# Mask, shift and two layer norms on GpSimd, one exponential per batch, bounds loaded between products, and an earlier second preparation, in a decoder layer on one core

## The reference

```
S1 = S + a (k^T S);  S2 = exp(log_f) S1;  S3 = S2 + a (k^T S2) + k v^T;  o = q^T S3
```

## Time and profile before

| | |
|---|---|
| median of 3 runs | 2480.19 us (2478.8 to 2481.66) |
| the profiled execution | 2477.74 us, span 2476.0 us |
| mean granted TensorE clock | 0.828 |
| VectorE busy | 2113.5 us, 85% |
| TensorE busy | 1768.9 us, 71% |
| GpSimd busy | 1016.9 us, 41% |
| ScalarE busy | 777.2 us, 31% |

### The profile page before, as it was taken

One profiled execution on the slowest core, in us unless ns is written; L12 is line 12 of the kernel. 1 busy time (PEld: TensorE's weight loads), 2 busy tenths in 40 slices (PEclk: granted clock), 3 DMA queues, 4 the chain that ended last, 5 costly groups with the idle time before them and its releaser, 6 DMA issues.

```text
span 2476.0 us, 32575 instructions
## 1 busy us (share of the span) xinstructions
PE 1768.9 (71%) x9438; PEld 1338.2 (54%) x9438; DVE 2113.5 (85%) x5985; ACT 777.2 (31%) x2209; POOL 1016.9 (41%) x1164
## 2 busy tenths in 40 slices
PE   4258887988798879877988330367887568857893
PEld 2145666667566656665667210245575446745683
DVE  5999999999999999999999989999999989941000
ACT  2142145314531453145313100252223511234121
POOL 2503350465046504550564467353663653231103
PEclk7558998999799979998999665567998669976997
DMA  8000342334233423332335120000353003530243
GB/s 270 18 1 14 127 135 74 112 136 137 77 119 124 135 77 127 116 135 80 120 121 179 45 76 9 20 1 3 102 200 128 18 2 121 204 116 1 98 165 111
DMA packets 175116, 238.57 MB, mean 96 GB/s; under 512 B 28657, under 2 KB 148074, under 8 KB 174954
## 3 DMA queue, kind: packets, MB, share of 16 engines
q1 hardware_dynamic: 140874, 194.46, 23.2%
q10 hardware_dynamic: 27936, 25.44, 3.2%
q0 software_dynamic: 6144, 16.79, 2.1%
HBM read 202.09 MB, written 33.16 MB: 95 GB/s over the span
## 4 chain that ended last, share of the span: by engine, by line
DVE 53%; PE 18%; POOL 10%; issue 8%; ACT 8%; DMA 2%; SPq 0%; ACTq 0%; POOLq 0%; DVEq 0%; PEldq 0%
DVE ps L1548 10%; DVE ps L1529 9%; DVE prod L1521 8%; DVE terms L1536 6%; ACT probs L820 4%; PE ps L629 4%; DVE terms L1531 4%; PE ps L620 3%; PE ps L573 2%; PE ps L566 2%; DVE rec_out L1477 2%; DVE rec_in L1477 2%; DVE SE_out L1540 1%; POOL in_rows L1021 1%; PE ps L523 1%
## 5 line engine op out<-in xcount | busy, mean ns | idle before, releaser
L1548 DVE TENSOR_REDUCE ps<-terms 128x64 f32<-128x320 f32 x1024 | 447.8, 482 | 0.0
L1529 DVE TENSOR_REDUCE ps<-prod 128x16 f32<-128x272 f32 x1024 | 396.5, 431 | 0.0
L620 PE MATMUL ps<-xg,fc 128*128 128x128 f32 x2848 | 361.4, 288 | 29.9 <-PE ps L629 12.5
L1536 DVE TENSOR_TENSOR terms<-ps,rec_out 128x256 f32<-128x256 f32 x1024 | 380.7, 413 | 0.0
L1521 DVE TENSOR_TENSOR prod<-ps,rec_in 128x256 f32<-128x256 f32 x1024 | 380.4, 412 | 0.0
L620 PEld LDWEIGHTS ps<-xg,fc 128*128 128x128 f32 x2848 | 350.4, 203 | 52.8 <-issue 44.4
L629 PE MATMUL ps<-pj,hT 128*128 128x256 f32 x1424 | 341.9, 395 | 34.5 <-ACT hT L901 34.5
L629 PEld LDWEIGHTS ps<-pj,hT 128*128 128x128 f32 x1424 | 271.0, 195 | 90.3 <-ACT hT L901 54.3
L1136 POOL TENSOR_TENSOR oprod<-SE_out,rec_q 128x320 f32<-128x320 f32 x171 | 147.3, 861 | 358.9 <-DVE SE_out L1540 357.8
L566 PE MATMUL ps<-xtf,fc 128*128 128x512 f32 x512 | 245.2, 618 | 6.9 <-ACT hT L852 3.5
L573 PE MATMUL ps<-pj,hT 128*128 128x256 f32 x1024 | 240.0, 386 | 0.0
(11 more groups left out here) (227 smaller groups left out, 2846.1 us busy)
## 6 DMA issues: line engine op xcount, KB each, us to landing
fc<-in_wfcT SPq DMA_DIRECT2D x80, 1024.0 KB, 5.2
pj<-in_wpT SPq DMA_DIRECT2D x80, 1024.0 KB, 8.4
xg_rows<-in_rows ACTq DMA_DIRECT2D x105, 128.0 KB, 2.1
out_rows<-y ACTq DMA_DIRECT2D x89, 128.0 KB, 5.7
in_rows<-o_rows SPq DMA_DIRECT2D x2, 2176.0 KB, 17.3
out_rows<-o_rows SPq DMA_DIRECT2D x2, 2176.0 KB, 17.1
xtp<-in_xT SPq DMA_DIRECT2D x32, 128.0 KB
xin<-in_x SPq DMA_DIRECT2D x8, 512.0 KB, 6.7
```

Source lines behind the costliest of these rows:

```text
L620: i = mm(ps[:, UP + g // 4, g % 4 * P:(g % 4 + 1) * P], fc[:, par, c, g * P:(g + 1) * P], xg[:, c], start=c == 0, stop=c == KC - 1)
L1529: red(SE[:, old, cols, HD:EH].rearrange("p v n -> p n v"), prod[:, c % PLACED, :, cols, 0:HD + 1], AX.X, ALU.add).then_inc(step_done, 1)
L1536: tt(terms[:, cols, :, 0:NV], SE[:, old, cols, HD:EH].unsqueeze(2).to_broadcast([P, HC, HD, NV]), rec_out[:, c].unsqueeze(1).to_broadcast( ...
L1548: red(SE[:, new, cols, 0:HD], terms[:, cols, :, 0:NV + 1], AX.X, ALU.add).then_inc(step_done, 1)
```

## The change

- In free tiles GpSimd does the first and second layer norm's subtraction and scaling (`normalize`) and masks the scores (`cap_scores`). The mask is now added (1e30 where masked, else 0) instead of a maximum with `cap`, so that the cap is made in one step.
- In tiles 0 to 4 and 7 (`SHIFTED`) GpSimd subtracts the row minimum (`shift_scores`), ScalarE takes one exponential per batch over all heads, and VectorE sums the rows (`sums_of_weights`). Tiles 5 and 6 keep 16 exponentials per batch.
- ScalarE's first exponential stands behind expert 6's passes in free tiles too.
- TensorE reads the bounds one at a time between products of the second shared expert (`edge_loads`).
- In free periods the second preparation comes before the projection, after `attT_sb` instead of `resid`, and the projection waits for `banks_read(3)`. In period 5 it comes before expert 8. GpSimd begins preparation operations of a period's second superblock at chunk 4 instead of 7.
- In the tail GpSimd shifts tile 7's scores before it gathers tile 6's rows. The due times in `FREE_AT` and `BOUND_AT` change.

The diff, without the lists of semaphores:

```diff
@@ -51,6 +51,8 @@
 FIRST_BOUND = O_FIRST // P
+LAST = TILES - 1
+SHIFTED = *range(FIRST_BOUND), LAST
@@ -60,15 +62,14 @@
-MASKED = 1e9 * QSCALE
-HUGE = 3e38
+MASKED = 1e30
...
-PREP_FROM, PREP_FROM_KEPT, PREP_FROM_SECOND, PREP_DONE_KEPT = 13, 5, 7, 29
+PREP_FROM, PREP_FROM_KEPT, PREP_FROM_SECOND, PREP_DONE_KEPT = 13, 5, 4, 29
@@ -294,7 +294,7 @@
                 sp.wait_ge(ln_out[LN_1], m * B)
-                sp.wait_ge(cap_half, m)
+                sp.wait_ge(cap_done, m)
@@ -303,7 +303,7 @@
             def store_tile(m):
-                sp.wait_ge(ln_out[LN_3], m * 2 + 2)
+                sp.wait_ge(ln_out[LN_3], m * B + B)
@@ -553,7 +553,7 @@
-            def shared(m, e, between=lambda: None):
+            def shared(m, e, between=lambda: None, late=lambda: None):
@@ -567,9 +567,11 @@
-                def down(g):
+                def down(g, behind=lambda: None):
...
                     for b in range(B):
+                        if b % 2 == 0:
+                            behind()
@@ -581,7 +583,7 @@
                 for g in range(4, FG):
-                    ins = down(g)
+                    ins = down(g, late)
@@ -589,12 +591,20 @@
-            def load_bounds(m):
-                pe.wait_ge(bounds_done, m + 1)
-                pe.sem_inc(bounds_seen_pe, 1)
-                edges = [pe.value_load(bounds[0:1, e:e + 1], min_val=0, max_val=TILES * MAX_ALL) for e in range(NR + 1)]
-                bounds_of_tile[m] = dict(zip(EXPERTS[NSH:], zip(edges, edges[1:])))
+            def edge_loads(m):
+                edges = []
+                def load():
+                    if not edges:
+                        pe.wait_ge(bounds_done, m + 1)
+                        pe.sem_inc(bounds_seen_pe, 1)
+                    e = len(edges)
+                    edges.append(pe.value_load(bounds[0:1, e:e + 1], min_val=0, max_val=TILES * MAX_ALL))
+                    if e == NR:
+                        bounds_of_tile[m] = dict(zip(EXPERTS[NSH:], zip(edges, edges[1:])))
+                return load
@@ -693,18 +703,21 @@
                     if m is not None:
-                        banks_read(1)
+                        banks_read(1 if bound else 3)
...
                         if m is not None:
-                            pe.wait_ge(resid, m * 2 + 2)
+                            pe.wait_ge(attT_sb, m * 2 + 2)
...
-                last_experts(f, (start, attend, weigh, finish, second))
+                def second_and_finish():
+                    second()
+                    finish()
+                last_experts(f, (start, attend, weigh, second_and_finish, lambda: None))
                 if m is not None:
-                    banks_read(1 if bound else 3)
@@ -712,13 +725,14 @@
                         banks_read(3)
-                    shared(m, 1)
+                    load = edge_loads(m)
+                    shared(m, 1, late=load)
+                    load()
...
                     own = EXPERTS[NSH:] if bound else EXPERTS[NSH:LATE]
-                    load_bounds(m)
@@ -815,6 +829,10 @@
             def exponentials(m, b):
+                if m in SHIFTED:
+                    act.wait_ge(shifted, SHIFTED.index(m) * B + (b + 1))
+                    fn(probs[:, b], probs[:, b], ACT.Exp, scale=-1.0).then_inc(exp_done, 1)
+                    return
@@ -944,15 +962,12 @@
                         scores(m)
-                        if not bound:
-                            exponentials(m, 0)
...
                     if m is not None:
-                        if bound:
-                            exponentials(m, 0)
+                        exponentials(m, 0)
@@ -963,7 +978,7 @@
-                hi = last_experts(f, (start, attend, weigh, lambda: None, second))
+                hi = last_experts(f, (start, attend, weigh, second, lambda: None))
@@ -1045,14 +1060,32 @@
-            def last_norm(m):
-                mv, rstd = ln_of[LN_3]
-                rsqrt(LN_3, m)
-                pool.wait_ge(ln_rstd[LN_3], m * 2 + 2)
-                tt(y_out[:, :], y_out[:, :], mv[:, :, 0].unsqueeze(2).to_broadcast([P, B, D]), ALU.subtract).then_inc(ln_out[LN_3], 1)
-                pool.wait_ge(ln_out[LN_3], m * 2 + 1)
-                tt(y_out[:, :], y_out[:, :], rstd[:, :].unsqueeze(2).to_broadcast([P, B, D]), ALU.mult).then_inc(ln_out[LN_3], 1)
+            def normalize(kind, m, src, dst):
+                mv, rstd = ln_of[kind]
+                rsqrt(kind, m)
+                tt(dst[:, :], src[:, :], mv[:, :, 0].unsqueeze(2).to_broadcast([P, B, D]), ALU.subtract).then_inc(ln_out[kind], B // 2)
+                pool.wait_ge(ln_rstd[kind], m * 2 + 2)
+                pool.wait_ge(ln_out[kind], m * B + B // 2)
+                tt(dst[:, :], dst[:, :], rstd[:, :].unsqueeze(2).to_broadcast([P, B, D]), ALU.mult).then_inc(ln_out[kind], B // 2)
+            def first_norm(m):
+                if m:
+                    pool.wait_ge(scattered, m * (MOVES * 16))
+                    pool.wait_ge(doubled, m)
+                normalize(LN_1, m, xin, x1)
+            def cap_scores(m, b):
+                pool.wait_ge(cap_done, m + 1)
+                pool.wait_ge(sc_sb, m * (2 * B) + (2 * b + 2))
+                tt(probs[:, b], probs[:, b], cap[:, b].unsqueeze(1).to_broadcast([P, H, SK]), ALU.add).then_inc(capped, 1)
+            def shift_scores(m, b):
+                pool.wait_ge(min_done, m * B + (b + 1))
+                tt(probs[:, b], probs[:, b], least[:, b].unsqueeze(2).to_broadcast([P, H, SK]), ALU.subtract).then_inc(shifted, 1)
@@ -1191,12 +1224,17 @@
                 if m is not None:
-                    jobs += [(at[LN_1] + 1, lambda: rsqrt(LN_1, m)), (at[LN_2] + 1, lambda: rsqrt(LN_2, m))]
+                    if bound:
+                        jobs += [(at[LN_1] + 1, lambda: rsqrt(LN_1, m)), (at[LN_2] + 1, lambda: rsqrt(LN_2, m))]
+                    else:
+                        jobs += [(at[LN_1] + 1, lambda: first_norm(m)), (at[LN_2] + 1, lambda: normalize(LN_2, m, x1, x2))]
+                        jobs += [(at["caps"], lambda b=b: cap_scores(m, b)) for b in range(B)]
+                        jobs += [(at["caps"], lambda b=b: shift_scores(m, b)) for b in range(B)]
...
                     jobs.append((at["combine"], lambda: combine(f)))
-                    jobs.append((at[LN_3] + 1, lambda: last_norm(f)))
+                    jobs.append((at[LN_3] + 1, lambda: normalize(LN_3, f, y_out, y_out)))
@@ -1211,17 +1249,19 @@
             rsqrt(LN_1, 7)
+            for b in range(B):
+                shift_scores(7, b)
...
             combine(6)
-            last_norm(6)
+            normalize(LN_3, 6, y_out, y_out)
...
             combine(7)
-            last_norm(7)
+            normalize(LN_3, 7, y_out, y_out)
@@ -1245,7 +1285,7 @@
                         nc.vector.bn_aggr(mv[:, b], stats[:, b]).then_inc(ln_mv[kind], 1)
-                if t == at + 1:
+                if t == at + 1 and dst is not None:
@@ -1261,10 +1301,7 @@
                     dve.wait_ge(mask_in, m * 16 + 16)
-                    nc.vector.tensor_scalar(cap[:, :, :], imask[:, :, :], 0.0, -HUGE, ALU.not_equal, ALU.mult).then_inc(cap_half, 1)
-                if t == 1:
-                    dve.wait_ge(cap_half, m + 1)
-                    nc.vector.tensor_scalar(cap[:, :, :], cap[:, :, :], MASKED, None, ALU.add).then_inc(cap_done, 1)
+                    nc.vector.tensor_scalar(cap[:, :, :], imask[:, :, :], 0.0, MASKED, ALU.is_equal, ALU.mult).then_inc(cap_done, 1)
@@ -1277,20 +1314,28 @@
-                for i in due(t, at, 2 * B, 2):
-                    b = i // 2
-                    if i % 2 == 0:
-                        dve.wait_ge(cap_done, m + 1)
-                        dve.wait_ge(sc_sb, m * (2 * B) + (2 * b + 2))
-                        tt(probs[:, b], probs[:, b], cap[:, b].unsqueeze(1).to_broadcast([P, H, SK]), ALU.max).then_inc(capped, 1)
-                    else:
+                for b in range(B):
+                    if t == at[b]:
+                        if m >= FIRST_BOUND:
+                            dve.wait_ge(cap_done, m + 1)
+                            dve.wait_ge(sc_sb, m * (2 * B) + (2 * b + 2))
+                            tt(probs[:, b], probs[:, b], cap[:, b].unsqueeze(1).to_broadcast([P, H, SK]), ALU.add).then_inc(capped, 1)
...
+            def sums_of_weights(t, m, at):
+                for b in range(B):
+                    if m in SHIFTED and t == at[b]:
+                        dve.wait_ge(exp_done, m * B + (b + 1))
+                        red(weight_sum[:, b], probs[:, b], AX.X, ALU.add).then_inc(summed, 1)
...
                     dve.wait_ge(exp_done, m * B + B)
+                    if m in SHIFTED:
+                        dve.wait_ge(summed, SHIFTED.index(m) * B + B)
@@ -1385,7 +1430,7 @@
                 caps(t, m)
-                if m and t == at[LN_1] + 1:
+                if bound and t == at[LN_1] + 1:
@@ -1393,12 +1438,13 @@
                 else:
```

(12 more changed lines are left out.)

5 lines of the change are left out of this document (2 added, 3 removed).

## The result

The kernel after takes **2462.21 us** (median of 4, 2461.71 to 2463.37) against 2480.81 of the kernel before beside it: ratio 0.9927, 95% interval 0.991 to 0.9944. It is 18.6 us faster, where 43 was forecast, and just outside the range.

The account below looks back on a forecast made before the run. VectorE, carrying the recurrence, was taken to bound the free periods, and tile 7's chain the tail. Free periods -28.4, period 5 -3, tiles 5 and 6's cap -0.6, tail -11: -43 from 2480.2, 2437 us, range 2418 to 2462.

Parts of the forecast that it names:

- stalls at x and rone: Free periods: VectorE waits for projection (x, residual sum) and router scores rt (rone, first routing operation), 17.2 us in all.
- It comes back at the lower clock for some 5 us: TensorE after its pause: projection takes 9.4 us, rt at S+39.1 (S is the lay-out's end), stall 3.2; low clock throughout, 6.4.
- Period 1 ... TensorE comes later without a pause: 0.9: Period 1 has two passes of expert 7, so TensorE arrives later without pausing and VectorE stalls only 0.9 us.
- Norms, -20.1: VectorE, five free periods: first and second normalization leave, 4 x 0.486 and 4 x 0.517 us a tile, 20.1 us less.
- The 2.6 us of waits for it go: GpSimd's combine comes earlier: VectorE's 2.6 us of waits go, plus 1.4 at period 4's kept lay-out, together 4.0.
- GpSimd ... I charge nothing: GpSimd's added 29 us a tile leaves 12 us of room before the lay-out, so no cost in the free periods.
- Masks -32.9: VectorE, five free periods: masking moves to GpSimd, 32.91 us less.
- only as room: TensorE then waits at `widened`: Free periods: TensorE's savings from fewer exponentials and bounds read singly become waiting at `widened`, so nothing is counted.
- Period 5 -3: Period 5: second preparation starts three chunks sooner, its four powers run before the gathers, 3 us less (0 to 6).
- Tail -11: Tail, tile 7 alone: 5 us less from `divided` starting sooner and 6 from the bounds, 11 in all (4 to 13).
- Rival B: Slow projection and exposed bound loads: -16 in the free periods, 0 in period 5, -4 in the tail; 2459 us, chance 0.2.
- Rival C: TensorE's clock stays low from pause to router, stall 15 us instead of 3.2 in four periods; 2494 us, chance 0.05.

Follow-up runs that it names:

- e6: The kernel after with unread TensorE products, cut to length, filling the pauses ahead of every tile's projection and 8 ahead of period 0's second preparation: 2423.0 us, ratio 0.9763.
- e4: The kernel after with unread TensorE products (9, 28, 26, 20) between second preparation and projection in periods 1 to 4: 2443.9 us, ratio 0.9843.
- e2: e1 with GpSimd beginning the second superblock's preparation at chunk 7 again instead of 4: 2454.3 us, ratio 0.9888.
- e12: e1 with VectorE's residual sum and second norm's statistics at t=67 instead of 71 (2422.8 us), plus free tiles' masks back on VectorE: 2459.3 us.
- e7: The kernel after with the nine bounds read in one go behind the second shared expert, as before: 2468.0 us, ratio 0.9949.
- e11: e9 with GpSimd's second preparation from chunk 7 in superblocks 1, 3, 5, 7, and unread products before the projections of tiles 5, 6, 7: 2405.8 us.
- e1: The kernel after with the old order restored in free periods, projection before expert 8 and second preparation behind `resid`: 2450.1 us, ratio 0.9865.
- e9: e1 with residual sum and second norm's statistics at t=67 instead of 71, and tile 6's last statistics behind `divided` in the tail: 2410.8 us.

## Why the prediction was wrong

The wait and the path were as forecast. What failed is the size of the stalls at x and rone, 17.2 in the forecast and 38.5 us measured, in two of its steps; three smaller terms were off as well. By its own steps:

- **"It comes back at the lower clock for some 5 us", projection 9.4.** It took 12.7, at the lower clock to its end. The 5 us were read from 5.88 us of an expert's products, and the projection did not come back as they did. A projection after a pause was there to be read, in the tail, where a batch's products took 2.08 us. The passes behind were 18.6 us against 17.5. In period 2 rt came at S+43.1 instead of S+39.1, and the stall was 4.9 + 1.6 = 6.5: the 6.4 that the text gave for "the low clock throughout". Periods 2 to 4 waited 6.5, 7.3 and 8.8 instead of 3.2, 3.2 and 4.6. In e6, where the pause is filled and the projection runs at full clock, period 2 waits 0.7, close to the 0.5 that the text gave for that case.
- **"Period 1 ... TensorE comes later without a pause: 0.9".** It paused 2.87 us and the projection took 12.7. The waits were 8.3 + 2.7 = 11.0. This is the largest single miss, 10.1 of the 21.3 us by which the stalls (38.5) exceed the 17.2. Period 0, worked out with a cold TensorE, was right: 4.9 against 5.3. e4 and e6 show how much of this is the clock's. In e6 period 1's projection starts at nearly the same place (7.7 us after the lay-out instead of 7.9), runs at full clock, and the period waits 2.1 + 0.7 = 2.8 us: so some 8 of the 10.1 are the clock's, and the other 2 that TensorE comes later than was reckoned.
- **Norms, -20.1.** The rows have means over free and bound tiles together. The 12 bound ones that are left in the kernel after, by line (busy us, mean ns):

```profile
L1291 DVE TENSOR_SCALAR x<-x,mv,rstd 128x256 f32<-128x256 f32 x12 | 7.6, 698 | 4.3 <-POOL rstd L1028 4.3
L1291 DVE TENSOR_SCALAR x<-xin,mv,rstd 128x256 f32<-128x256 f32 x12 | 6.3, 586 | 4.5 <-POOL rstd L1028 4.5
```

The bound tiles have the longer ones. The 40 that went had taken 14.1 us, as the view of the kernel before says for L1251 in its free periods (window, length, busy and count of VectorE, then clock, DMA share, GB/s):

```profile
54.20:1295.90 1241.70, 14.11 (x40) 0.87 0.30 101
```

That is 6.0 less than the 20.1 taken. Two readings failed here. Their own means were 421 and 409 ns and not the group's 486 and 517, which makes 16.6 of the 20.1. And four of them in a row overlap, so that 40 times the mean is more than the time they are busy, 14.1.

- **"The 2.6 us of waits for it go", -4.0.** Of this term only the lay-out's 1.4 us went. VectorE still waits 2.5 us for combine in the free periods, at once in period 4 (stats at L1283 above).
- **"GpSimd ... I charge nothing".** Lay-out, minima and sums never waited for it, as said. But the preparation put earlier fell beside routing: +1.5 in period 1 and +1.9 in 2 and 3, while in period 4 the routing operations lost 2.3. Net 3.1. What the prediction said of the recurrence held: a chunk's period stayed 3.0 us. That routing's operations with two SBUF inputs fall under the other half of the Trainium skill's rule, as the prediction cites it, was not weighed. And its short form there, that an instruction with a single SBUF input does not contend, was too wide: L1413 and L1418 in the rows of e2 read one and grew.
- The sum for the free periods then closes within 3 us: the forecast's part without the new stalls was -33.3 - 4.0 - 8.3 = -45.6; with norms +6.0, combine +2.5, routing +3.1 and stalls +38.5 it gives +4.5, and +2.2 was measured. What the other 2.3 are was not found.
- **Masks -32.9.** Right: the masks are gone from VectorE's rows, the first superblocks became 17.7 us shorter, and e12 gives 30 to 37 us for them.
- **ScalarE and the bounds, "only as room: TensorE then waits at `widened`".** Right, 8.34 us of waiting in period 2, and e7 shows that the room from the bounds was worth less than nothing in the free periods (3.2 us). The loads between products were hidden but for 0.94 us.
- **Period 5 -3:** -5.9, its waits for the output terms went from 12.6 to 6.3. **Tail -11:** -12.3; the bounds gave 8.1 for 6, which leaves 4.2 for the attention part (2.4 by e7's tail of 420.6), for 5.

Rival B had the slow projection and came nearest, 2459, but that is luck: the loads were hidden and not exposed, and its -16 for the free periods was +2.2. Rival C, the clock low up to the router, fell: the second expert pass and the router ran at full clock (3.83 and 1.06 us). The +50 in C's sum is four times 11.8 us, which is 47; nothing hangs on the difference.

## What to carry to other kernels

Where one engine's order is written by due times, time saved on another does not come back but collects as pauses in front of those due times; look where each saved microsecond will stand idle, and move the due times with it (here two numbers gave 1%). A pause of some microseconds on TensorE can cost the speed of what follows it, here 6 us a projection, so put nothing that is needed soon behind a wait for another engine, and read the price from the same operation after a pause, not from another. A mean over a group of rows must not be used for a part of the group, nor a count times a mean where the operations overlap.

## What the runs showed of the hardware

- After a pause of 8.67 us, and in period 1 after 2.87, TensorE worked on without a gap for 12.7 us at 1.2 GHz (granted clock 0.50); an expert's products behind it came back to 2.4 GHz in their first pass (4.42 us against 3.73 in period 2).
- After shorter pauses it went both ways. Behind 0.61 us the projection took 6.8 us in 21 cases and 10.2 to 10.7 in 7, where it fell from 2.4 to 1.2 GHz in its second batch; behind 1.52 (e11) and 1.76 us (e6) of pause it did the same. A preparation behind 1.37 us (e1) ran at full clock, and in the tail, behind attention work, the projection was slow after 1.74 us (e9).
- With unread products through the pause the granted clock was 1.00, over 12.2 us of them and the 6.65 us of the projection behind (e4).
- VectorE operations on 8 to 72 elements that took 0.15 to 0.50 us in e2 took 0.59 to 0.98 beside a GpSimd product of 512 elements; a reduction took 0.23 both times.
- GpSimd took 2.58 us for a mask of 1232 elements and 2.4 for a shift with a broadcast, and VectorE's recurrence kept its pace (3.01 us a chunk in the free periods, before and after). One exponential of 1232 elements took 1.23 us on ScalarE, against 16 of 0.35 with a reading of 0.19 each.
